# The norms beside a wide attention stage, cut in halves and shared between VectorE, ScalarE and GpSimd

## The chip, the cores and the metric

The kernel runs on one core of one Trainium2 chip. The metric is the device time of one execution in microseconds, the median of several.

## The reference, cut to what matters

The program is a stack of four layers, each an attention and a feed-forward part, over 4 batches of 1024 tokens with 128 channels. The change lies in the last attention (16 heads of 64 channels, "wide") and in what runs beside it:

```
x  = layernorm(x + moe_out(x))          # end of layer 2: inner norm with g2, be2, then + x and a norm
# layer 3 attention
Q, K, V = x @ Wq.T + bq, x @ Wk.T + bk, x @ Wv.T + bv      # 16 heads of 64
w  = softmax(Q K^T * SCALE * adaptive_scale)
y  = x + (w V) @ Wo.T + bo
y  = (y - mean(y)) / sqrt(var(y) + eps) * gamma + beta
x  = layernorm(x + y)
# layer 3 feed-forward: gates by 25 bisection steps over 8 expert logits, then 8 experts
```

So every batch passes two norms before wide attention (inner with g2 and be2, outer after the sum with x) and two after it (inner with gamma and beta, outer after the sum with x).

## The kernel before, in words

`wide_attention` (L3997) treats 32 units, one for each batch and pair of heads; unit u is batch u // 8, pair u % 8. A unit is eight key tiles (kb 0 to 7). All engines walk one list of steps, `plan`, and each executes those that concern it, in the list's order. For each tile and each half of the queries TensorE multiplies scores (L4210 adds the negative maximum, L4213 keys by queries), ScalarE takes the exponential (L4348) into one of six buffers, TensorE weighs the values with it (L4227), and VectorE and GpSimd add up the exponentials of one half each (both L4144). Beside that TensorE computes bf16 scores of the next unit (L3915), of which VectorE takes maxima (`max`, L3946), 16 a unit: three in tiles 0 and 2, two in the others, none in tile 7. In tile 7 the maxima are joined (L3954), transposed by TensorE (L3922), split in a high and a low part (L3959, L3961) and sent by SyncE as a row (`send`). Score, maximum and several other steps share three pairs of PSUM banks in turn, so TensorE waits until the step three places earlier has been read. The next unit but one is projected in tile 6 (q: L3980 on ScalarE, then a cast L3929 on VectorE) and tile 7 (k; v: L3936 on VectorE). Tile 1 holds the sums, tile 3 a reciprocal (L4284), tile 5 the divide (L4279) of the unit before.

GpSimd's add of a tile is placed beside the next tile's first maximum (`add_beside`), since VectorE's maximum reads PSUM.

Three kinds of side work are put into that list:

- `later`: when a batch is finished, its output projection (`rows`, two steps of 32 products each, L249; L256 and L259 on VectorE), its own norms (`stats_1`, `root_1`, `scale_1` in two halves, `affine` three times, `stats_2`, `root_2`, `scale_2` in halves), the turns (four transposes L225, a copy L230), and for batch 0 the routing. One step is taken from it in tiles 0, 2, 4, 6 and 7.
- `rest`: the norms of the layer before for batches 1 to 3 (`Tail.steps`) and, for batches 2 and 3, the gathering of the experts' rows (GpSimd's indirect DMAs, L3285) and their combination (L3298). One step in tiles 2, 4 and 6.
- `work`: the 215 small gate instructions of batch 0, two in each tile once the routing has run (L3750 to L3811).

A norm is eight `bn_stats` and eight `bn_aggr` (`stats_on_dve`, L147, instructions L152 and L155), a reciprocal root by three Newton steps, eleven small instructions (`root_on_dve`, L189), and eight `tensor_scalar` of 128x128 (`scale_on_dve`, L207, instruction L211), all on VectorE. Between the two norms of a batch come three 128x1024 instructions, times gamma, plus beta, plus x: L4307, L4311, L4315 for wide attention's own, L3339, L3342, L3345 for the layer before. Where the steps stand is set by hand:

```
            plan += gate_work(IN_TILE)
            ...
            else:
                plan += next_later()
            if kb in (2, 4, 6) and rest:
                plan.append(rest.pop(0))
```

## Time and profile before

| | us |
|---|---|
| median of 3 runs | 5788.23 (5783.87 to 5794.31) |
| profiled execution | 5795.58, its span 5793.8 |
| TensorE busy | 5261.2, 91% of the span |
| VectorE busy | 4089.6, 71% |
| ScalarE busy | 2696.3, 47% |
| GpSimd busy | 1227.6, 21% |
| granted TensorE clock, mean | 0.946 |
| wide stage, first to last exponential | 3666 to 5239 |

Busy time counts what an engine executes; waits, semaphores and DMA issues are not in it. The shares are means over stages that have different limits, so they say little of the wide stage. In the trace, a row of the timeline gives start and length in us, the engine (DVE is VectorE, ACT ScalarE, POOL GpSimd, PE TensorE), the line, and in brackets how long the engine sat idle before and what released it.

### The profile page before, as it was taken

How to read it: one execution, taken by the hardware profiler on the slowest of the kernel's cores; microseconds unless marked ns; L12 is line 12 of the kernel's file. 1: busy time of each engine (PE TensorE's matmuls, PEld its weight loads, DVE VectorE, ACT ScalarE, POOL GpSimd, SP SyncE). 2: the span in 40 equal slices, each digit the busy share in tenths (PEclk: the TensorE clock that was granted, in tenths of full speed). 3: DMA queues.
4: the chain of work that ended last, by engine and by line, in shares of the span. 5: the costliest groups of instructions: out<-in, count | busy, mean ns of one | idle time of the engine just before them, and what ended most of it. 6: DMA issues, size and time to landing. Idle time of an engine off the chain costs nothing. (4 is left out here: it accounts for less than half of the span.)

```text
span 5793.8 us, 86268 instructions
## 1 busy us (share of the span) xinstructions
PE 5261.2 (91%) x31277; PEld 2629.9 (45%) x31277; DVE 4089.6 (71%) x7068; ACT 2696.3 (47%) x4526; POOL 1227.6 (21%) x859
## 2 busy tenths in 40 slices
PE   6999998787999999989999978899898899997999
PEld 2333333344567777772222248333333333334676
DVE  7888886774677777768898944677787877763412
ACT  4656665221233333337776756444344344442333
POOL 0110100220112322321102203244343233331000
PEclk7999998787989999999999999999999999998999
DMA  4211110002111111112111122000000000001000
GB/s 88 46 31 30 31 30 11 0 0 61 36 33 23 37 23 30 25 23 38 31 31 34 39 60 78 26 16 16 12 19 9 12 12 12 12 12 37 5 4 8
DMA packets 148359, 156.96 MB, mean 27 GB/s; under 512 B 48980, under 2 KB 95108, under 8 KB 147508
## 3 DMA queue, kind: packets, MB, share of 16 engines
q1 hardware_dynamic: 143336, 142.37, 11.3%
q0 software_dynamic: 4096, 8.40, 0.5%
q8 instruction: 250, 4.10, 0.3%
q14 instruction: 173, 1.42, 0.1%
q10 hardware_dynamic: 504, 0.69, 0.1%
HBM read 118.20 MB, written 37.40 MB: 27 GB/s over the span
## 5 line engine op out<-in xcount | busy, mean ns | idle before, releaser
L3946 DVE TENSOR_REDUCE wide_max_parts<-wide_p 128x2 f32<-128x1024 f32 x496 | 592.9, 1218 | 127.9 <-PE wide_p L3915 117.8
L759 ACT ACTIVATE attn_w<-l_p 128x512 f32<-128x512 f32 x1024 | 549.3, 596 | 276.0 <-DVE l_p L1203 152.0
L2518 PE MATMUL caus_p<-caus_x_one,big 128*128 128x129 f32 x4608 | 642.7, 287 | 0.0
L610 DVE TENSOR_REDUCE l_max_parts<-l_p 128x2 f32<-128x1024 f32 x512 | 602.1, 1219 | 46.8 <-PE l_p L586 42.4
L2602 ACT ACTIVATE big<-caus_p 128x512 f32<-128x512 f32 (+3 forms) x768 | 345.9, 489 | 576.7 <-PE caus_p L2504 418.5
L610 DVE TENSOR_REDUCE rot_max_parts<-rot_p 128x2 f32<-128x1024 f32 x488 | 574.1, 1219 | 51.1 <-PE rot_p L586 48.6
L2518 PEld LDWEIGHTS caus_p<-caus_x_one,big 128*128 128x128 f32 x4608 | 592.8, 199 | 35.7 <-issue 2.6
L4213 PE MATMUL wide_p<-arena 64*128 64x512 f32 x2048 | 538.0, 604 | 0.0
L4348 ACT ACTIVATE attn_w<-wide_p 128x1024 f32<-128x1024 f32 x342 | 350.4, 1024 | 390.6 <-PE wide_p L4213 387.1
L4144 POOL TENSOR_TENSOR big<-big,attn_w 128x1024 f32<-128x1024 f32 x128 | 333.5, 2606 | 454.5 <-PE wide_p L3915 442.2
L610 DVE TENSOR_REDUCE caus_max_parts<-caus_p 128x2 f32<-128x1024 f32 (+2 forms) x360 | 340.5, 956 | 24.2 <-PE caus_p L586 15.9
L739 PE MATMUL l_p<-l_q_stack,l_k_stack 98*128 98x512 bf16 x1024 | 336.6, 387 | 13.4 <-ACT attn_w L759 9.6
L4227 PE MATMUL wide_p<-attn_w,arena 128*64 128x512 f32 x1368 | 333.8, 609 | 0.0
L2636 POOL TENSOR_TENSOR attn_w<-attn_w,caus_part 128x256 f32<-128x256 f32 x256 | 186.3, 728 | 685.5 <-DVE caus_part L2578 685.5
L759 ACT ACTIVATE attn_w<-rot_p 128x512 f32<-128x512 f32 x512 | 275.9, 595 | 110.3 <-PE rot_p L739 110.1
L739 PE MATMUL rot_p<-arena 98*128 98x512 bf16 x1024 | 316.1, 389 | 8.1 <-DVE rot_max_lo L638 1.9
L759 ACT ACTIVATE big<-rot_p 128x512 f32<-128x512 f32 x512 | 274.5, 599 | 77.9 <-PE rot_p L739 75.7
L3244 ACT ACTIVATE arena<-moe_experts,moe_b 128x512 f32<-128x512 f32 x256 | 175.3, 687 | 271.3 <-PE moe_experts L3232 271.2
L769 PE MATMUL l_p<-attn_w,l_v_one 128*32 128x512 f32 x2048 | 277.4, 614 | 0.0
L3265 DVE SCALAR_TENSOR_TENSOR x_mid<-moe_experts,last_gates,x_mid 128x128 f32<-128x128 f32 x256 | 72.1, 344 | 279.5 <-PE moe_experts L3254 279.5
L4348 ACT ACTIVATE wide_exps<-wide_p 128x1024 f32<-128x1024 f32 x170 | 174.2, 1024 | 190.9 <-PE wide_p L4213 188.1
L4210 PE MATMUL wide_p<-wide_max_rows,wide_ones_bf 64*128 64x512 bf16 x1024 | 201.6, 390 | 57.0 <-DVE wide_max_parts L3946 50.2
(625 smaller groups left out, 8957.4 us busy)
## 6 DMA issues: line engine op xcount, KB each, us to landing
arena<-q_parts SPq DMA_DIRECT2D x576, 32.0 KB
arena<-k_parts SPq DMA_DIRECT2D x576, 32.0 KB
arena<-inverse_rows SPq DMA_DIRECT2D x64, 256.0 KB
l_q_stack<-q_parts SPq DMA_DIRECT2D x279, 32.0 KB
l_k_stack<-k_parts SPq DMA_DIRECT2D x279, 32.0 KB
q_parts<-arena SPq DMA_DIRECT2D x8, 768.0 KB, 3.6
k_parts<-arena SPq DMA_DIRECT2D x8, 768.0 KB, 3.6
attn_w<-moe_in SPq DMA_DIRECT2D x19, 256.0 KB
```

What stands on the lines that cost most here:

```text
L610: self.nc.vector.tensor_reduce(self.max_parts[:, 2 * p:2 * p + 2, n, half], pair[:, :, 0:self.width(n, half)], AX.X, ALU.max).then_inc(*se ...
L739: mm = nc.tensor.matmul(bank, heads.k_stack[i][0:STACK, j, kb * P:(kb + 1) * P], heads.q_stack[i][0:STACK, j, half * BANK:(half + 1) * BAN ...
L759: self.nc.scalar.activation(self.exps[t % len(self.exps)], bank, ACT.Exp).then_inc(*self.exped.up())
L769: mm = self.nc.tensor.matmul(self.out[self.W * j:self.W * (j + 1), :], self.v_one[u % 2][:, kb, j, :], self.exps[(t + j) % len(self.exps)] ...
L2518: mm = nc.tensor.matmul(outs[o % 2][:, nq % 2 * (C + 1):(nq % 2 + 1) * (C + 1)], exps[h % 2][:, kb, nq * P:(nq + 1) * P], x_one[b % 2][:, ...
L2602: nc.scalar.activation(exps[h % 2][:, kb, lo:BANK], bank[:, lo:BANK], ACT.Exp).then_inc(*exped.up())
L3946: self.nc.vector.tensor_reduce(self.max_parts[:, :, n, h], side, AX.X, ALU.max).then_inc(*self.maxed.up())
L4144: calls.tensor_tensor(to, first, exps[t % E_BUFS], ALU.add).then_inc(*summed[h].up())
L4210: nc.tensor.matmul(side[:, a, :], heads.ones_bf[own[a], :], max_rows[u % 2][own[a], cols], start=True, stop=False)
L4213: mm = nc.tensor.matmul(side[:, a, :], k[u % SLOTS][own[a], kb * P:(kb + 1) * P], q[u % SLOTS][own[a], cols], start=False, stop=True)
L4227: mm = nc.tensor.matmul(out[own[a], h, :], v_tok[u % SLOTS][:, kb, own[a]], exps[t % E_BUFS][:, a, :], start=kb == 0, stop=kb == NT - 1)
L4348: nc.scalar.activation(exps[t % E_BUFS], side, ACT.Exp).then_inc(*exped.up())
```

## The change

All of it is in the wide stage. Batch 3's own norms at the end of the stage are left as they were.

1. `stats_on_dve` can do half of a norm's eight tiles. A list `steps` marks each half as heavy; heavy steps are taken only at two places of a unit: in tile 6 ahead of `project_q`, and in tile 7 between `project_k` and `project_v`.
2. The root stays on VectorE, with one instruction more, which makes `shift` = -mean * rstd. It is taken in tile 0.
3. The scaling goes to ScalarE: `activation(Identity, bias=shift, scale=rstd)`, four 128x128 tiles in tile 2 and four in tile 3.
4. Times gamma, plus beta, plus x go to GpSimd, in tiles 4 and 5 and in tile 0 of the next unit.
5. A norm or a pair of combinations so takes one unit and the next one's first tiles; `rest` is now a list of jobs, in which a batch's own norms stand behind more urgent ones (a job is one batch's; light steps are taken in tiles 0 to 5).
6. The routing of batch 0 moves from unit 11 to unit 14, the gates run beside units 14 to 29, two in each of tiles 0 to 6 and none in tile 7. Gathers stand in tiles 0 and 1, combinations in tiles 6 and 7. `rows` stands in tiles 6 and 7 as before.

```diff
-    def stats_on_dve(self, v, c, src):
+    def stats_on_dve(self, v, c, src, part=None):
         nc = self.nc
-        if c:
+        tiles = range(NT) if part is None else range(part * NT // 2, (part + 1) * NT // 2)
+        if c and part != 1:
             v.wait_ge(*self.out_done.at(NT * c))
-        for i in range(NT):
+        for i in tiles:
...
+class LateNorms:
...
+    def steps(self, b):
+        out = []
+        for second in range(2):
+            out += [(True, ("n_stats", self.tag, b, second, part)) for part in range(2)]
+            out += [(False, ("n_root", self.tag, b, second)), (False, None)]
+            out += [(False, ("n_scale", self.tag, b, second, part)) for part in range(2)]
+            if second == 0:
+                out += [(False, ("n_affine", self.tag, b, i)) for i in range(3)]
+        return out + [(False, ("n_turn", self.tag, c)) for c in range(HALF * b, HALF * (b + 1))]
...
+    def stats_on_dve(self, v, b, second, part, ready):
+        if part == 0:
+            v.wait_ge(*(self.affine.at(3 * b + 3) if second else ready))
+        self.norm.stats_on_dve(v, 2 * b + second, self.x_of(b) if second else self.x1(b), part)
+
+    def root_on_dve(self, v, b, second):
+        norm, c = self.norm, 2 * b + second
+        norm.root_on_dve(v, c)
+        v.wait_ge(*norm.rooted.at(norm.PER_ROOT * (c + 1)))
+        self.nc.vector.scalar_tensor_tensor(self.shift[:, :], norm.mv[:, :, 0], -1.0, norm.rstd[:, :], ALU.mult,
+                                            ALU.mult).then_inc(*self.shifted.up())
+
+    def scale_on_act(self, a, b, second, part):
+        rows = self.x_of(b) if second else self.x1(b)
+        if part == 0:
+            a.wait_ge(*self.shifted.at(2 * (b - self.first) + second + 1))
+        for i in range(part * NT // 2, (part + 1) * NT // 2):
+            self.nc.scalar.activation(rows[:, i, :], rows[:, i, :], ACT.Identity, bias=self.shift[:, i:i + 1],
+                                      scale=self.norm.rstd[:, i:i + 1]).then_inc(*self.norm.out_done.up())
+
+    def affine_on_pool(self, pool, b, i):
...
+        if i == 0:
+            pool.wait_ge(*self.norm.out(2 * b))
+        else:
+            pool.wait_ge(*self.affine.at(3 * b + i))
...
+        self.nc.gpsimd.tensor_tensor(out, one, other, op).then_inc(*self.affine.up())
...
+    def next_step(heavy):
+        while rest and not rest[0]:
+            rest.pop(0)
+        if not rest or rest[0][0][0] != heavy:
+            return []
+        step = rest[0].pop(0)[1]
...
+            if kb == NT - 1:
+                more = u + 2 < len(units)
+                plan += [("project_k", u + 2)] * more + next_step(True) + [("project_v", u + 2)] * more
...
+                if kb == NT - 2:
+                    plan += next_step(True) + [("project_q", u + 2)] * (u + 2 < len(units))
...
-            plan += gate_work(IN_TILE)
+            if kb < NT - 1:
+                plan += gate_work(IN_TILE)
+            if kb < NT - 2:
+                plan += next_step(False)
...
-            else:
-                plan += next_later()
-            if kb in (2, 4, 6) and rest:
-                plan.append(rest.pop(0))
+            if kb >= NT - 2 and ends:
+                plan.append(ends.pop(0))
```

VectorE from the end of one unit into the next, where the first norm of batch 2 of the layer before begins. Before, in units 7 and 8 (L3954 joins the maxima, L3936 writes the values, L3946 are maxima, L4144 adds):

```order
L3929 CAST wide_q_bf<-arena 128x1024
L152 BN_STATS tail_stats<-x_mid 128x6 x8
L155 BN_AGGR tail_mv<-tail_stats 128x2 x8
L3954 TENSOR_REDUCE wide_neg_max<-wide_max_parts 128x16
L3959 CAST wide_max_hi<-wide_p 16x128
L3961 TENSOR_TENSOR wide_max_lo<-wide_p,wide_max_hi 16x128
L3936 TENSOR_TENSOR arena<-wide_p,wide_bv 128x1024
L4144 TENSOR_TENSOR big<-big,attn_w 128x1024
L3946 TENSOR_REDUCE wide_max_parts<-wide_p 128x2 x5
```

With the change, in units 6 and 7 (lines of the changed file: L3991 is the cast, L4016 the join, L3998 the values, L4008 the maxima, L194 the root's first instruction):

```order
L153 BN_STATS tail_stats<-x_mid 128x6 x4
L156 BN_AGGR tail_mv<-tail_stats 128x2 x4
L3991 CAST wide_q_bf<-arena 128x1024
L4016 TENSOR_REDUCE wide_neg_max<-wide_max_parts 128x16
L4021 CAST wide_max_hi<-wide_p 16x128
L4023 TENSOR_TENSOR wide_max_lo<-wide_p,wide_max_hi 16x128
L153 BN_STATS tail_stats<-x_mid 128x6 x4
L156 BN_AGGR tail_mv<-tail_stats 128x2 x4
L3998 TENSOR_TENSOR arena<-wide_p,wide_bv 128x1024
L4216 TENSOR_TENSOR big<-big,attn_w 128x1024
L4008 TENSOR_REDUCE wide_max_parts<-wide_p 128x2 x3
L194 TENSOR_SCALAR tail_std<-tail_mv 128x8
```

The statistics moved from behind the cast, ahead of the join, to ahead of the cast and behind the split; the root follows tile 0's three maxima, where before it stood behind the maxima and the add of tile 2 of unit 8.

GpSimd in units 7 and 8, in which before there are only its adds (L4144) at this place. With the change (L4216 are the adds, L3412 gamma, beta and the sum):

```order
L4216 TENSOR_TENSOR big<-big,attn_w 128x1024
L4216 TENSOR_TENSOR big<-big,wide_exps 128x1024
L3412 TENSOR_TENSOR x_mid<-x_mid,tail_g 128x1024
L4216 TENSOR_TENSOR big<-big,attn_w 128x1024
L3412 TENSOR_TENSOR x_mid<-x_mid,tail_be 128x1024
L4216 TENSOR_TENSOR big<-big,attn_w 128x1024
L4216 TENSOR_TENSOR big<-big,wide_exps 128x1024
L4216 TENSOR_TENSOR big<-big,attn_w 128x1024
L3412 TENSOR_TENSOR x_tok<-x_tok,x_mid 128x1024
```

Three instructions of VectorE now stand between GpSimd's adds, the first two each behind the add of a tile in the middle of the unit.

## Rows read from the trace of the kernel before

Unit u's first tile is counted from its first exponential.

**Rows 1.** Stretches: length, each engine's busy time (instructions), PEclk, DMA share, GB/s.

```profile
3705.99:5070.74 1364.75, 1262.81 (x6524) 492.44 (x6524) 1057.24 (x1481) 581.82 (x579) 525.07 (x221) 0.97 0.05 13
3847.91:4025.74 177.83, 174.21 (x900) 63.61 (x899) 134.69 (x138) 85.20 (x85) 88.89 (x42) 1.00 0.07 18
4741.07:4784.91 43.84, 43.55 (x225) 15.90 (x225) 33.78 (x47) 21.30 (x22) 17.84 (x7) 1.00 0.05 13
4910.14:4939.05 28.91, 28.91 (x199) 20.82 (x197) 11.02 (x18) 7.42 (x7) 6.04 (x3) 1.00 0.01 2
5070.74:5158.03 87.29, 87.20 (x451) 31.93 (x450) 63.49 (x60) 42.60 (x42) 34.96 (x14) 1.00 0.05 13
```

**Rows 2.** Who TensorE waited for in units 1 to 27: us, times, longest.

```profile
PE wide_p L4210 <- DVE wide_max_parts L3946: 48.3, 21, 4.4
PE wide_p L3922 <- DVE wide_neg_max L3954: 32.1, 23, 3.4
```

**Rows 3.** VectorE, unit 28 and into 29: start, us, instruction [idle time before, releaser].

```profile
5100.35 1.22 DVE L4144 TENSOR_TENSOR big<-big,attn_w 128x1024 f32<-128x1024 f32 x1
...
5106.05 1.22 DVE L4279 TENSOR_TENSOR arena<-arena 128x1024 f32<-128x1024 f32 x1
5107.19 2.38 DVE L3946 TENSOR_REDUCE wide_max_parts<-wide_p 128x2 f32<-128x1024 f32 x2
...
5113.36 0.69 DVE L3929 CAST wide_q_bf<-arena 128x1024 bf16<-128x1024 f32 x1 [2.66 <-ACT arena L3980]
...
5118.19 1.23 DVE L3936 TENSOR_TENSOR arena<-wide_p,wide_bv 128x1024 f32<-128x1024 f32 x1 [3.00 <-PE wide_p L3901]
...
5126.44 1.23 DVE L3946 TENSOR_REDUCE wide_max_parts<-wide_p 128x2 f32<-128x1024 f32 x1 [1.32 <-PE wide_p L3915]
```

**Rows 4.** GpSimd in the same unit, in order of time.

```profile
5097.95 2.36 POOL L4144 TENSOR_TENSOR big<-big,wide_exps 128x1024 f32<-128x1024 f32 x1 [2.21 <-PE wide_p L3915]
...
5109.63 3.28 POOL L4144 TENSOR_TENSOR big<-big,wide_exps 128x1024 f32<-128x1024 f32 x1
```

**Rows 5.** VectorE in units 7 and 8: a statistics step and a root.

```profile
4025.32 1.64 DVE L152 BATCH_NORM_STATS2 tail_stats<-x_mid 128x6 f32<-128x128 f32 x8
4026.87 0.62 DVE L155 BATCH_NORM_AGGREGATE tail_mv<-tail_stats 128x2 f32<-128x6 f32 x8
...
4051.73 0.17 DVE L193 TENSOR_SCALAR tail_std<-tail_mv 128x8 f32<-128x8 f32 x1
...
4052.14 2.30 DVE L199 TENSOR_TENSOR tail_square<-tail_rstd 128x8 f32<-128x8 f32 x1
...
4055.97 2.35 DVE L3946 TENSOR_REDUCE wide_max_parts<-wide_p 128x2 f32<-128x1024 f32 x2
```

**Rows 6.** ScalarE between the exponentials of tiles 3 and 4, unit 28.

```profile
5097.70 1.02 ACT L4348 ACTIVATE attn_w<-wide_p 128x1024 f32<-128x1024 f32 x1 [2.25 <-PE wide_p L4213]
```

**Rows 7.** Stretches: tile 4 of unit 8; tiles 1 to 3 of units 9 and 28.

```profile
4053.08:4059.83 6.75, 4.64 (x26) 1.55 (x24) 6.48 (x13) 2.05 (x3) 2.37 (x2) 1.00 0.00 0
4102.65:4118.17 15.52, 15.48 (x86) 5.00 (x84) 13.88 (x29) 7.74 (x8) 4.71 (x3) 1.00 0.01 3
5078.90:5094.42 15.52, 15.47 (x86) 5.01 (x84) 11.88 (x11) 7.74 (x8) 4.71 (x3) 1.00 0.01 2
```

**Rows 8.** Groups of instructions, xcount | busy us, mean ns | idle before (whole span; PE units 1 to 27).

```profile
L3155 POOL TENSOR_TENSOR x_mid<-x_mid,rot_g 128x1024 f32<-128x1024 f32 x4 | 9.4, 2348 | 296.9 <-DVE x_mid L211 296.9
...
L1856 ACT ACTIVATE lin_o_scale<-lin_o_scale,lin_eps 128x128 f32<-128x128 f32 x4 | 1.6, 402 | 10.0 <-DVE lin_o_scale L1718 10.0
...
L225 PE MATMUL wide_p<-ident,x_tok 128*128 128x128 f32 x48 | 7.5, 283 | 0.3 <-DVE wide_max_parts L3946 0.3
L1988 PE MATMUL wide_p<-wide_w_router,x_chn 128*128 128x8 f32 x16 | 1.8, 251 | 0.0
```

**Rows 9.** GpSimd and VectorE side by side in unit 11, in order of time.

```profile
4239.51 2.74 POOL L4144 TENSOR_TENSOR big<-big,wide_exps 128x1024 f32<-128x1024 f32 x1
...
4239.95 3.38 DVE L4279 TENSOR_TENSOR arena<-arena 128x1024 f32<-128x1024 f32 x1
```

More of the change, by code:

```diff
@@ L4037, in wide_attention, with gathered @@
     IN_TILE = 2
-    work, later, rest = [], [], tail.steps(1)
-    for b in range(2, nb):
-        chunks = [c for c, (route, at) in enumerate(back.chunks) if (route.first_tile + at) // NT == b]
-        rest += [("gather", chunks[0])]
-        for c in chunks:
-            rest += [("gather", c + 1)] if c < chunks[-1] else []
-            rest += [("none",), ("combine", c)]
-        rest += tail.steps(b)
+    mine = LateNorms(st, "own", norm, turn, gamma[:, :], beta[:, :], affine, lambda b: mid, 0)
+    moe = LateNorms(st, "moe", tail.norm, tail.turn, tail.g2[:, :], tail.be2[:, :], tail.affine,
+                    lambda b: core.x_mid[:, b * NT:(b + 1) * NT, :], 1)
+    norms = {"own": mine, "moe": moe}
+    def gathered(b):
+        first = [c for c, (route, at) in enumerate(back.chunks) if (route.first_tile + at) // NT == b][0]
+        return [(heavy, (kind, first + c)) for heavy, kind, c in (
+            (False, "gather", 0), (False, "gather", 1), (True, "combine", 0), (True, "combine", 1),
+            (False, "gather", 2), (False, "gather", 3), (True, "combine", 2), (True, "combine", 3))]
+    work, ends, later = [], [], []
+    rest = [moe.steps(1)] + [gathered(b) + moe.steps(b) for b in range(2, nb)]
     def gate_work(n):
@@ L4103, in wide_attention @@
                     finish(units[u - 1][0])
-            else:
-                plan += next_later()
-            if kb in (2, 4, 6) and rest:
-                plan.append(rest.pop(0))
-    while work or later:
-        plan += gate_work(1) + next_later()
+            if kb >= NT - 2 and ends:
+                plan.append(ends.pop(0))
+    assert not work and not any(rest) and not ends
     last = len(units) - 1
@@ L4113, in wide_attention @@
     finish(nb - 1)
-    while later:
-        plan += next_later()
+    plan += ends + later
     plan = with_banks(plan, 3, {
@@ L4120, in wide_attention @@
         "turn": lambda c: (turn.kept, c + 1),
-        "tail_turn": lambda c: (tail.turn.kept, c + 1),
+        "n_turn": lambda tag, c: (norms[tag].turn.kept, c + 1),
         "route": lambda: (entmax.router.done, 1), **heads.released()})
@@ L4325, in _ @@
                     back.on_dve(v, *args)
-                elif kind == "tail":
-                    b = args[1]
-                    tail.on_dve(v, *args, back.combined.at(NT * (b - 1)))
+                elif kind == "n_stats":
+                    tag, b, *part = args
+                    norms[tag].stats_on_dve(v, b, *part, rows.out(2 * b + 1) if tag == "own" else
+                                            back.combined.at(NT * (b - 1)))
+                elif kind == "n_root":
+                    norms[args[0]].root_on_dve(v, *args[1:])
                 elif kind == "route":
```

55 lines of the change are left out of this document (34 added, 21 removed).

## Prediction

> **What bounds the kernel now.** I read the trace by stretches of the wide stage first. One attention unit (one batch, one pair of heads) is eight key tiles, and the stage is 32 units. Units 28 and 29, beside which no norm, gate or gather runs, take 87.29 us with TensorE busy for 87.20 of it, so the floor is 43.65 us a unit and TensorE sets it [rows 1]. Units 1 to 27, beside which all the side work lies, take 1364.75 us, where 27 x 43.65 = 1178.6 would do: **186.2 us** over the floor. What ends TensorE's waits there is VectorE: 48.3 us for the maxima that free a score bank and 32.1 for the joined maximum of the next unit [rows 2]. TensorE's busy time is also above its floor, 1262.8 against 27 x 43.6 = 1177.2, partly extra matmuls, partly the granted clock: 0.97 over these units, 1.00 in the clean ones [rows 1]. So VectorE's queue, not its 77% of busy time, is what to look at.
>
> The clean unit tells where VectorE has room [rows 3]. It has none between the divide and the maxima of tile 6 (5107.19, with no idle time before them), but before the cast of q in tile 6 it sits idle for 2.66 us, before the values of tile 7 for 3.00, and before the first maximum of tile 1 for 1.32. Before the change the norm steps lie in tiles 2, 4 and 6, or behind the cast: in unit 7 the statistics (1.64 and 0.62) stand between the cast and the join [rows 5], so TensorE's transpose of the join comes as much later.
>
> **What can't go.** The projections of one batch (the rows step) take 28.91 us where the two tiles that hold them take 6.26 + 8.16 = 14.42 in a clean unit (tiles 7 and 0: of 43.65, tiles 1 to 3 take 15.52 [rows 7] and tiles 4 to 6 three times 4.57, which is how far the adds at 5100.35 and 5104.92 stand apart, the second being 1.13 ahead of the divide [rows 3]): 14.5 us of TensorE's own, three times, 43.5 [rows 1]. Twelve turns are 48 transposes of together 7.5 us, of which I count 7.0, and the router's matmuls are 1.8 [rows 8]. That is 52.3. **186.2 - 52.3 = 133.9 us** is what side work costs the stage now, and the most that the change can bring.
>
> **The change, part by part.**
> - *Statistics in halves*, in 12 units, before the cast in tile 6 and before the values in tile 7. Half of 1.64 + 0.62 is 1.13 us [rows 5], under 2.66 and 3.00 [rows 3]. They read one SBUF tensor, and their 8 instructions took 1.64 whoever else ran. Cost 0; without that cover it would be 24 x 1.13.
> - *Root* in tile 0, 12 times: eleven small instructions of 0.17 and one more for the shift, at a pitch of 0.20, 2.4 us. The idle time behind is 1.32, so tile 1's maxima come 1.1 us late (1.5 where two gate steps stand ahead). TensorE bears that: the root of unit 8 held VectorE from 4051.73 to 4055.97, 4.2 us, and the tile that followed took 6.75 in place of 4.57 [rows 5, 7], so about 2.0 us of lateness are free. And statistics of 2.3 us at just this place in unit 9 cost nothing, its tiles 1 to 3 taking 15.52 as in unit 28 [rows 7]. Cost 0, bound 12 x 0.4.
> - *The root's neighbours.* In unit 8 one instruction of the root took 2.30 us and not 0.17, because a GpSimd add ran beside it [rows 5]. In tile 0 GpSimd's add ends before the third maximum does. No such wait.
> - *Scaling on ScalarE*, four instructions in tile 2 and four in tile 3. The nearest row (128x128, SBUF to SBUF) has 0.40 each, 1.6 in all [rows 8]; between two tiles' exponentials ScalarE idles 2.25 us [rows 6]. Cost 0. VectorE loses 96 such instructions.
> - *Gamma, beta and sum on GpSimd*, in 6 units: two in tiles 4 and 5, one in the next unit's tile 0. The same instructions ran there in an earlier stage at 2.35 us [rows 8]. Here is the price. GpSimd's add of tile 4 ends at 5100.31, and behind it the new instruction starts 0.14 later; VectorE's add begins at 5100.35 and so is first [rows 3, 4]. Where both want the second SBUF input, one stands still: GpSimd's add of 5109.63 took 3.28, that is 2.2 after VectorE's ended [rows 4], and a divide that began beside GpSimd took 3.38, until 1.1 after it [rows 9]. With these two: gamma ends 5103.8; GpSimd's add 3.9 to 6.3; VectorE's add, due at 5104.92, ends 7.4; beta, waiting since 6.4, goes ahead of the divide and ends 9.6; the divide ends 10.7; tile 6's maxima start 3.4 us late. Less the 2.0 that are free, **1.4 us** in each of units 1, 7 and 11. In units 17, 21 and 26 two gate steps stand behind each add, and one of them waits out one more instruction, 2.3 to 2.6: 6.0 late, 4.0 lost, and some at a lower clock, 5. Together 3 x 1.4 + 3 x 5 = **19 us**. Bounds: nothing below (gathers that put GpSimd as far behind in units 4 to 7 cost 3.2 us in 177.83, so near 0 is possible), and above 12 instructions that each hold VectorE twice for 2.3, less 6 x 2: 43. I take the worked value, since its two durations are rows of exactly this meeting. The third, in tile 0, starts behind GpSimd's add when VectorE is on maxima, which read PSUM: 0.
> - *Combines* in tiles 6 and 7, eight in pairs. Units 4 to 7 now lose 177.83 - 174.6 = 3.2 us to three of them [rows 1]. The four in tile 7 lie in the 3.00; the four in tile 6 stand before the cast but behind GpSimd's long add: 0.8 each, **3 us** (0 to 4.3).
> - *Gates*: none in tile 7, same number. Unit 21 has two in each tile and takes 43.84, so 0.19 over 15.5 units, **3 us** (0 to 6).
> - *Gathers* in tiles 0 and 1, where GpSimd idles; in unit 14 one slips to tile 2: **2 us** (0 to 4).
>
> - *The new waits.* ScalarE's first scaling waits for the root's shift; behind it stand the exponentials, and for them TensorE. The shift is made two tiles earlier (tile 0 against 2), so it would have to be over 5 us late to be felt. GpSimd's gamma waits for the last scaling, one tile before; behind it stand GpSimd's own adds, and an exponential waits for those only six buffers, three tiles, on. TensorE's turn waits for the scaling of the tile before, due some 4 us ahead. Cost 0 each, as long as the roots stay in tile 0; SyncE's queue is not touched.
>
> Sum: 133.9 - 19 - 3 - 3 - 2 = 107 us less. The profiled execution took 5795.6, so 5688.6; it stands 7.4 above the median of the three runs, so against that median I forecast **5681 us**.
>
> The Trainium skill (GPSIMD Engine Reference, its summary of when to use which engine) says that two-input elementwise work belongs on VectorE, GpSimd being about twice as slow. The trace agrees on the ratio, 2.35 against 1.22 [rows 3, 8]. By that rule the move of 18 instructions would be a loss of 18 x 1.13 = 20 us and not a gain; an estimate, and one that holds only where GpSimd is waited for, which here it is only through the shared input.
>
> **The rivals.**
> - *GpSimd is never in the way* (13%). If the new instruction always loses the race and VectorE's next add comes after it, the price of 19 falls to about 0: 5788.2 - 133.9 + 8 = 5662. For it: VectorE starts 0.1 us earlier in the row. Against: in rows 9 the instruction that had waited went first. The Trainium skill (SBUF — State Buffer, "Who interferes with whom") has whoever issues first hold the shared pair for its whole instruction; that would give VectorE the first add and GpSimd the turn after it, which is the forecast's chain.
> - *The blocking spreads* (17%). Both bounds are reached, 43 + 4 + 6 + 4 and 5 for the roots: 62, so 5788.2 - 72 = 5716. For it: in the gated units two more steps stand behind each add, and VectorE once late stays beside GpSimd. Against: units 4 to 7.
> - *The excess was not the norms'* (4%). Gates and combines alone, in units 12 to 14, would be what is slow; then half stays: 5788.2 - 67 = 5721.
> - *Slower* (4%). Each of the 18 GpSimd instructions holds two adds in turn, and the add held on GpSimd's side makes the next tile's late too, three tiles on: if that costs 9 us per instruction, 162, then 5788.2 - 134 + 8 + 162 = 5824. It decides from 7 us per instruction on ((134 - 8) / 18). Against: a single wait is 2.3 us, and there is 2.66 + 3.00 of idle time twice a unit to recover in.
>
> **How the numbers follow.** Forecast 62%, the others 13, 17, 4 and 4. The range takes in the first two rivals and nearly the third: 5655 to 5722. A measurement of this kernel can tell 0.2%, 11.6 us, from no change. Faster by more than that: 0.93; within: 0.03; slower: 0.04.
>
> **What would show it.** Right: units with only statistics, roots and scaling near 43.7 to 44; TensorE's wait for the join and for maxima below 25 us together, and the granted clock near 1.00 in the stage; VectorE's divide stretched to 3 us in units 1, 7, 11, 17, 21 and 26 and nowhere else; four activations of 0.4 us or less between exponentials. Wrong: stretched adds in units without gamma and beta; an exponential that waits for GpSimd; statistics in tile 6 that delay the cast; tile 1 longer than 4.98 us behind a root.

## The result, and the profile after the change

The changed kernel takes **5696.59 us** (median of 4 runs, 5692.06 to 5699.48), the kernel before on the same chip 5791.27 (4 runs, 5783.87 to 5795.12): ratio 0.984, 95% interval 0.9827 to 0.9853, or 94.7 us less. The profiled execution took 5694.58, its span 5692.8. The forecast was 5681.

Runs of this kernel also differ ahead of the wide stage: its first exponential came between 3648.4 and 3678.8 us in the profiled executions of this study, with the same instructions ahead of it. So beside the times I compare the **stage** alone: from the first exponential of its first tile to the first exponential of its last. It took 1568.43 us before and takes 1475.27 now, 93.2 less. That is nearly all of the 94.7.

Units are cut at the first exponential of their first tile from here on. Those of [rows 1] were cut one exponential earlier, at the last of the unit before, because the load of the activation table had been counted as the first. For sums over units that matters little: before, units 1 to 27 are 184.2 us over the floor of 43.65 a unit by the right cut, where the prediction had 186.2.

Stretches of the changed kernel: units 1 to 27; unit 2; units 14 and 15; unit 17; units 28 and 29 (length, busy time of each engine and instructions, granted clock, DMA share, GB/s).

```profile
3704.09:4975.19 1271.10, 1237.43 (x6517) 482.32 (x6515) 1001.73 (x1357) 614.71 (x665) 565.26 (x239) 0.99 0.05 14
3750.16:3793.81 43.65, 43.61 (x228) 15.96 (x225) 33.87 (x46) 21.30 (x22) 19.79 (x8) 1.00 0.04 13
4297.80:4399.72 101.92, 92.70 (x469) 34.50 (x467) 85.09 (x103) 42.61 (x43) 55.03 (x30) 0.97 0.09 22
4457.85:4508.13 50.28, 45.37 (x228) 16.36 (x225) 43.76 (x57) 24.36 (x30) 22.37 (x9) 0.97 0.04 11
4975.19:5063.85 88.66, 88.33 (x460) 32.71 (x458) 68.11 (x93) 46.84 (x53) 34.93 (x14) 1.00 0.05 13
```

Units 1 to 27 take 1271.10 where [rows 1] had 1364.75: 92.6 over the floor. The granted clock rose from 0.97 to 0.99. Unit 2, which has the sum of a norm in its tile 0 and the statistics of the next in tiles 6 and 7, stands exactly on the floor. Apart from what can't go, what is left sits in few places: unit 17 is 6.6 over the floor, units 14 and 15 together 14.6 (1.9 of that is the router).

Who TensorE waited for in units 1 to 27 (us in total, times, longest).

```profile
PE wide_p L4282 <- DVE wide_max_parts L4008: 17.0, 7, 3.8
PE wide_p L3984 <- DVE wide_neg_max L4016: 8.1, 17, 1.0
PE wide_p L3968 <- DVE wide_max_parts L4008: 7.3, 5, 2.4
```

The first two answer to [rows 2]: the wait for maxima fell from 48.3 to 17.0, that for the join from 32.1 to 8.1 and from 3.4 to 1.0 at the longest. The third, a wait of the projections, was 17.0 before.

VectorE from unit 0 into unit 1: a whole norm's statistics in two halves, then the root.

```profile
3693.85 0.47 DVE L153 BATCH_NORM_STATS2 tail_stats<-x_mid 128x6 f32<-128x128 f32 x2
...
3696.19 0.69 DVE L3991 CAST wide_q_bf<-arena 128x1024 bf16<-128x1024 f32 x1 [1.60 <-ACT arena L4042]
...
3697.95 0.85 DVE L153 BATCH_NORM_STATS2 tail_stats<-x_mid 128x6 f32<-128x128 f32 x4
...
3701.03 1.23 DVE L3998 TENSOR_TENSOR arena<-wide_p,wide_bv 128x1024 f32<-128x1024 f32 x1 [1.94 <-PE wide_p L3963]
...
3704.30 3.66 DVE L4008 TENSOR_REDUCE wide_max_parts<-wide_p 128x2 f32<-128x1024 f32 x3 [0.91 <-PE wide_p L3977]
3707.87 0.16 DVE L194 TENSOR_SCALAR tail_std<-tail_mv 128x8 f32<-128x8 f32 x1
...
3710.08 0.17 DVE L3393 SCALAR_TENSOR_TENSOR wide_shift_moe<-tail_mv,tail_rstd 128x8 f32<-128x8 f32 x1
3710.16 2.35 DVE L4008 TENSOR_REDUCE wide_max_parts<-wide_p 128x2 f32<-128x1024 f32 x2
```

The halves lie in idle time: of 2.66 us before the cast 1.60 is left, of 3.00 before the values 1.94 [rows 3]. The root runs from 3707.87 to 3710.16 without a stretched step (in [rows 5] one took 2.30), and the next exponentials stand 4.98 and 5.56 us apart (3709.07, 3714.63) as in a clean unit. On ScalarE the scaling takes 1.64 for four:

```profile
3715.92 1.02 ACT L4423 ACTIVATE attn_w<-wide_p 128x1024 f32<-128x1024 f32 x1 [0.27 <-PE wide_p L4285]
3716.84 1.64 ACT L3401 ACTIVATE x_mid<-x_mid,wide_shift_moe,tail_rstd 128x128 f32<-128x128 f32 x4
3719.61 1.02 ACT L4423 ACTIVATE wide_exps<-wide_p 128x1024 f32<-128x1024 f32 x1 [1.13 <-PE wide_p L4285]
```

The exponential behind it still waits 1.13 for TensorE, so the scaling costs nothing.

**Where it does cost.** GpSimd in unit 1, tiles 3 to 6, with gamma at 3726.75 and beta at 3732.36 (L3412):

```profile
3724.43 2.36 POOL L4216 TENSOR_TENSOR big<-big,wide_exps 128x1024 f32<-128x1024 f32 x1 [2.21 <-PE wide_p L3977]
3726.75 2.35 POOL L3412 TENSOR_TENSOR x_mid<-x_mid,tail_g 128x1024 f32<-128x1024 f32 x1
3729.06 3.35 POOL L4216 TENSOR_TENSOR big<-big,attn_w 128x1024 f32<-128x1024 f32 x1
3732.36 3.44 POOL L3412 TENSOR_TENSOR x_mid<-x_mid,tail_be 128x1024 f32<-128x1024 f32 x1
3735.76 3.33 POOL L4216 TENSOR_TENSOR big<-big,attn_w 128x1024 f32<-128x1024 f32 x1
3739.23 3.27 POOL L4216 TENSOR_TENSOR big<-big,wide_exps 128x1024 f32<-128x1024 f32 x1
```

VectorE beside it:

```profile
3726.83 3.35 DVE L4216 TENSOR_TENSOR big<-big,attn_w 128x1024 f32<-128x1024 f32 x1
...
3732.37 1.21 DVE L4216 TENSOR_TENSOR big<-big,attn_w 128x1024 f32<-128x1024 f32 x1
3733.50 3.38 DVE L4351 TENSOR_TENSOR arena<-arena 128x1024 f32<-128x1024 f32 x1
3736.81 2.34 DVE L4008 TENSOR_REDUCE wide_max_parts<-wide_p 128x2 f32<-128x1024 f32 x2
...
3741.34 1.72 DVE L3991 CAST wide_q_bf<-arena 128x1024 bf16<-128x1024 f32 x1 [1.05 <-ACT arena L4042]
```

Gamma starts 0.04 us before the end that its predecessor shows, and 0.08 ahead of VectorE's add at 3726.83. That add then takes 3.35 in place of 1.22, until 1.1 after gamma's end. VectorE's next add begins 0.01 behind beta, and this time it is beta that stands still (3.44 in place of 2.35); but the divide behind that add begins while beta still runs, and takes 3.38, until 1.1 after beta's end. So tile 6's maxima start at 3736.81, 3.1 us late by the distances of [rows 3], and tile 6 is 1.5 us longer.

The unit is 2.4 over the floor, though. The other 0.9 is in tile 7 and comes through something that the prediction did not have: GpSimd's add of tile 6, at 3739.23, now lies beside VectorE's cast of q, which takes 1.72 in place of 0.69, and the join stands behind the cast. The cast is held in units 1, 7 and 11 and in no other unit; in the kernels below in which it takes 0.69 there, tile 7 is on the floor.

In a gated unit (17) two gate steps of 0.2 us stand behind the late add, and each is held as well. At 1.22 and 0.2 each the three would be over some 1.6 us after 4480.58, near 4482.2; the maxima start at 4488.39, 6.2 late, and tile 5 is 4.5 us longer. The divide is held behind that (3.37), and tile 6 is another 1.9 longer.

```profile
4480.58 3.35 DVE L4216 TENSOR_TENSOR big<-big,wide_exps 128x1024 f32<-128x1024 f32 x1
4483.85 2.32 DVE L3863 COPY_PREDICATED wide_ent_low<-wide_ent_keep,wide_ent_mid 128x8 f32<-128x8 uint32 x1
4486.21 2.26 DVE L3849 TENSOR_SCALAR wide_ent_width<-wide_ent_width 128x8 f32<-128x8 f32 x1
4488.39 2.34 DVE L4008 TENSOR_REDUCE wide_max_parts<-wide_p 128x2 f32<-128x1024 f32 x2
```

TensorE stands still behind them, and its next matmuls of scores take 1.61 for four. In unit 2, where the granted clock is 1.00, they take 1.02 (at 3750.38); over unit 17 it is 0.97.

```profile
4489.66 0.39 PE L4282 MATMUL wide_p<-wide_max_rows,wide_ones_bf 64*128 64x512 bf16 x2 [3.83 <-DVE wide_max_parts L4008]
4489.89 1.61 PE L4285 MATMUL wide_p<-arena 64*128 64x512 f32 x4
```

The second dear place is unit 14, where four gathers stand ahead of GpSimd's adds and the first gates stand in VectorE's queue. GpSimd, then VectorE:

```profile
4317.60 0.94 POOL L3286 DMA_INDIRECT x_mid<-moe_out,sort_index  x1 [0.30 <-issue]
4318.56 2.71 POOL L4216 TENSOR_TENSOR big<-big,attn_w 128x1024 f32<-128x1024 f32 x1
```

```profile
4318.99 2.31 DVE L3841 TENSOR_TENSOR wide_ent_width<-wide_ent_high,wide_ent_low 128x8 f32<-128x8 f32 x1
...
4325.67 2.38 DVE L3816 SCALAR_TENSOR_TENSOR wide_ent_power<-wide_ent_diff 128x64 f32<-128x64 f32 x1
...
4331.62 2.33 DVE L3845 TENSOR_SCALAR wide_ent_f_low<-wide_ent_f_low 128x8 f32<-128x8 f32 x1
```

The gathers push GpSimd's add from beside a maximum (which reads PSUM) to beside a gate step (which reads SBUF); 0.2 us of work becomes 2.3, VectorE is late by then, and the pair meets again in each of the next tiles. The first meeting costs TensorE nothing; then tiles 4, 5 and 6 are 0.5, 1.4 and 4.1 us longer.

### The profile page after: what moved, and what is told of

Same layout as the page of the kernel before. It is cut to its first block and busy times, and to the rows that moved or that the text cites. A ratio compares the mean times of both kernels' runs of the same rounds, so it can differ in the third digit from the quotient of the medians.

```text
span 5692.8 us, 86280 instructions
## 1 busy us (share of the span) xinstructions
PE 5238.4 (92%) x31277; PEld 2622.7 (46%) x31277; DVE 4035.5 (71%) x6966; ACT 2733.3 (48%) x4622; POOL 1266.8 (22%) x877
## 5 line engine op out<-in xcount | busy, mean ns | idle before, releaser
L4008 DVE TENSOR_REDUCE wide_max_parts<-wide_p 128x2 f32<-128x1024 f32 x496 | 595.4, 1220 | 129.5 <-PE wide_p L3977 117.4
L4216 POOL TENSOR_TENSOR big<-big,attn_w 128x1024 f32<-128x1024 f32 x128 | 331.8, 2592 | 391.9 <-PE wide_p L3977 379.4
L611 DVE TENSOR_REDUCE caus_max_parts<-caus_p 128x2 f32<-128x1024 f32 (+2 forms) x360 | 340.6, 956 | 24.2 <-PE caus_p L587 15.9
L740 PE MATMUL l_p<-l_q_stack,l_k_stack 98*128 98x512 bf16 x1024 | 336.9, 388 | 12.8 <-ACT attn_w L760 9.0
L2637 POOL TENSOR_TENSOR attn_w<-attn_w,caus_part 128x256 f32<-128x256 f32 x256 | 186.2, 727 | 681.9 <-DVE caus_part L2579 681.9
L3233 PE MATMUL moe_experts<-x_chn,big 128*128 128x512 f32 x512 | 237.1, 606 | 14.0 <-ACT arena L3245 8.8
```

The costliest lines, as they stand in the source:

```text
L611: self.nc.vector.tensor_reduce(self.max_parts[:, 2 * p:2 * p + 2, n, half], pair[:, :, 0:self.width(n, half)], AX.X, ALU.max).then_inc(*se ...
L740: mm = nc.tensor.matmul(bank, heads.k_stack[i][0:STACK, j, kb * P:(kb + 1) * P], heads.q_stack[i][0:STACK, j, half * BANK:(half + 1) * BAN ...
L3233: self.nc.tensor.matmul(self.up_banks[o % 3], self.w1[:, e, c * P:(c + 1) * P], cols, start=True, stop=True).then_inc(*self.up_mm.up())
L4008: self.nc.vector.tensor_reduce(self.max_parts[:, :, n, h], side, AX.X, ALU.max).then_inc(*self.maxed.up())
L4216: calls.tensor_tensor(to, first, exps[t % E_BUFS], ALU.add).then_inc(*summed[h].up())
```

## The experiments

Ten kernels, each the changed kernel with one edit (or, the best one, three). All in one table; the stage and the excess over the floor in units 1 to 27 are of the profiled execution, the ratio is to the kernel before on the same chip, with its 95% interval.

The kernels did not all run on one chip (the kernel before had medians of 5788.76, 5788.93 and 5791.64 beside the later ones), and most of the intervals overlap. So I compare these kernels with each other by the stage, unit by unit. That is one profiled execution of each, but units that an edit does not touch agree to 0.05 us in nearly all cases. The exceptions are unit 5 (up to 0.2), units 14 and 15, which together lie between 14.3 and 15.9 over the floor in kernels that are edited elsewhere, and the last two units. Differences between stages of up to 1.5 us therefore mean nothing.

| kernel | median us | ratio | stage us | units 1 to 27 |
|---|---|---|---|---|
| before | 5791.27 | | 1568.43 | 184.2 |
| changed | 5696.59 | 0.984 (0.9827 to 0.9853) | 1475.27 | 92.6 |
| gamma, beta, sum on VectorE | 5685.21 | 0.9828 (0.9797 to 0.9859) | 1465.23 | 82.5 |
| all three in tile 0 of the next unit | 5680.52 | 0.9821 (0.979 to 0.9852) | 1462.95 | 80.5 |
| gates from unit 16 on | 5687.63 | 0.9828 (0.9796 to 0.986) | 1463.05 | 80.4 |
| clearings in place of gamma and beta | 5670.57 | 0.9802 (0.9761 to 0.9843) | 1451.45 | 68.7 |
| scaling on VectorE | 5753.63 | 0.9945 (0.9923 to 0.9966) | 1534.03 | 144.4 |
| tile 6's half behind the cast | 5704.0 | 0.9859 (0.9827 to 0.9892) | 1489.54 | 105.8 |
| statistics whole, ahead of the cast | 5703.17 | 0.9858 (0.9825 to 0.9891) | 1475.09 | 92.4 |
| spare tensor_scalar on VectorE | 5773.39 | 0.9972 (0.9956 to 0.9987) | 1547.64 | 158.8 |
| spare bn_stats on VectorE | 5708.9 | 0.9874 (0.9811 to 0.9938) | 1486.43 | 101.3 |
| best | 5654.79 | 0.9775 (0.9754 to 0.9797) | 1437.98 | 55.3 |

### What do gamma, beta and the sum cost, and through what?

**Back on VectorE**, in the same tiles.

```diff
-        self.nc.gpsimd.tensor_tensor(out, one, other, op).then_inc(*self.affine.up())
+        self.nc.vector.tensor_tensor(out, one, other, op).then_inc(*self.affine.up())
```

> The change with one part undone: gamma, beta and the sum run on VectorE again, at the same places of the list (tiles 4 and 5, tile 0 of the next unit); halves of statistics and ScalarE's scaling stay. In the changed kernel the six units with these steps and the tile behind them take 25 us over the floor of 43.65 a unit. Theory A (VectorE waits for GpSimd at the shared second SBUF input): each instruction costs VectorE 1.13 us of its own, 2.3 in tiles 4 and 5 together, little more than the 2.0 us of lateness that TensorE bears; so 0 to 1 us in units 1, 7 and 11 and 1 to 3 in units 17, 21 and 26, about 8 in all, and the kernel 17 us faster than the changed one, ratio 0.981 to before. Theory B (VectorE is full in these tiles, whoever holds it up): 1.13 us more work costs as much as a wait; no faster than the changed kernel, ratio 0.984.

Measured: 1.7 us each in units 1, 7 and 11, and 4.0, 3.9 and 3.7 in the gated units 17, 21 and 26 (16.5 in all) where the GpSimd version has 26.1. Twice what I expected, yet 10 less than on GpSimd. In unit 17 of this kernel neither add is held; only the divide, at 4478.37, meets GpSimd's add and takes 3.39. The meeting happens once and not twice, and no gate step stands in it. The same one is left in the other five units (in unit 1 the divide, at 3726.80, takes 3.38).

**All three in tile 0 of the next unit**, still on GpSimd, back to back behind its add.

```diff
-                out += [(False, ("n_affine", self.tag, b, i)) for i in range(3)]
+                out += [(False, None)] * 2 + [(False, ("n_affine", self.tag, b))]
...
-                    norms[args[0]].affine_on_pool(pool, *args[1:])
+                    for i in range(3):
+                        norms[args[0]].affine_on_pool(pool, args[1], i)
```

> All three of gamma, beta and the sum stay on GpSimd but stand together in tile 0 of the next unit, where GpSimd idles about 8 us behind its add and VectorE mostly reads PSUM; tiles 4 and 5 hold none. Theory A: three instructions are 7.2 us and end before tile 2; VectorE's only two-input work there is the add of tile 1 and, in units 18, 22 and 27, gate steps. Cost 0 in units 2, 8 and 12, up to 1 us in the gated ones; 25 us of excess shrink to under 4, the kernel about 21 us faster than the changed one (5696.6), ratio 0.980. Theory B: the same amount of work on GpSimd costs the same wherever it stands, 25 us, ratio 0.984.

Measured: 0 in the ungated units (1, 2, 7, 8, 11 and 12 stand on the floor), but 4.2 to 4.4 in each of the units 18, 22 and 27, where gates run. The stage lost 12.3 us, not the 21 expected. In unit 18 VectorE reads:

```profile
4501.44 3.28 DVE L4216 TENSOR_TENSOR big<-attn_w 128x1024 f32<-128x1024 f32 x1
4504.64 2.34 DVE L3863 COPY_PREDICATED wide_ent_low<-wide_ent_keep,wide_ent_mid 128x8 f32<-128x8 uint32 x1
4507.01 0.17 DVE L3849 TENSOR_SCALAR wide_ent_width<-wide_ent_width 128x8 f32<-128x8 f32 x1
```

and GpSimd beside it:

```profile
4501.27 2.36 POOL L3412 TENSOR_TENSOR x_tok<-x_tok,x_mid 128x1024 f32<-128x1024 f32 x1
4504.60 2.35 POOL L4216 TENSOR_TENSOR big<-attn_w 128x1024 f32<-128x1024 f32 x1 [0.97 <-PE wide_p L3977]
```

In a gated unit the add of tile 1 begins 0.17 after the sum and is held until 1.1 after it; then a gate step, begun 0.04 after GpSimd's add, is held for the whole of that. The add is held as long in the ungated units 2, 8 and 12 (3.24 us each), which stand on the floor, and in units 18, 22 and 27 of the best version below (3.2 to 3.3), which has no gates at that place and loses 0.2 to 0.3 there. What costs 4 us is the gate step held behind it.

**Clearings in place of gamma and beta.** GpSimd writes zeros over the rows for about as long (1.96 and 0.52 us) and reads nothing; the inner norm's result is zero in this kernel, and the sum stays.

```diff
+        if i < 2:
+            for rows in (x1, x1):
+                self.nc.gpsimd.memset(rows, 0.0).then_inc(*self.cleared.up())
+                pool.wait_ge(*self.cleared.now())
+            self.nc.gpsimd.memset(x1[:, 0:NT // 2, :], 0.0).then_inc(*self.affine.up())
+            return
```

> A measurement, with part of the computation changed: times gamma and plus beta (tiles 4 and 5) are replaced by two and a half clearings of the same 128x1024 rows on GpSimd, so that the inner norm's output is zero. GpSimd is busy about as long (2 x 0.95 + 0.5 us, plus two waits on itself, some 2.6 in place of 2.35), but reads no SBUF. The sum in tile 0 is left. Theory A (shared read): VectorE's add in tile 4 takes 1.22 and not 3.35, the divide 1.22 and not 3.38; what is left is GpSimd's own adds, 0.3 to 0.6 us late. Excess of the six places 25 us to under 6. Theory B (GpSimd's queue is late): GpSimd's adds start as late as in the changed kernel, VectorE waits for them, and the excess stays above 15 us.

Measured: units 1, 7 and 11 on the floor, units 17, 21 and 26 at 0.2 to 0.3, the gates' own price: 25.3 us gone in these six units, 23.8 in the stage. GpSimd in unit 1 is as late as before:

```profile
3728.25 1.96 POOL L3415 MEMSET x_mid<- 128x1024 f32 x2
3730.27 0.52 POOL L3417 MEMSET x_mid<- 128x512 f32 x1
3730.76 2.36 POOL L4223 TENSOR_TENSOR big<-big,attn_w 128x1024 f32<-128x1024 f32 x1
```

and VectorE's adds, one of which lies wholly beside the clearings, are short:

```profile
3728.35 1.22 DVE L4223 TENSOR_TENSOR big<-big,attn_w 128x1024 f32<-128x1024 f32 x1
...
3732.91 1.29 DVE L4223 TENSOR_TENSOR big<-big,attn_w 128x1024 f32<-128x1024 f32 x1
```

So it is reading SBUF that costs; GpSimd's longer queue by itself costs nothing. This is what the Trainium skill (SBUF — State Buffer, "Who interferes with whom") states of a VectorE instruction with two SBUF inputs: it contends with a GpSimd instruction that reads, not with one that only writes.

### Why are units 14 and 15 dear?

The gates begin in unit 16, behind the gathers and combines that stand in units 14 and 15, still two a tile, and end in unit 31.

```diff
-            if kb < NT - 1:
+            if kb < NT - 1 and u >= 16:
                 plan += gate_work(IN_TILE)
```

> The gates of batch 0 begin in unit 16 and not in unit 14, still two a tile, and so run into unit 31; nothing else moves. In the changed kernel units 14 and 15, where gates, gathers and combinations meet, lie 13.6 us over the floor, 1.9 of it the router. If the cost is that meeting (each small gate step waits 2.3 us for a GpSimd that the gathers made late), units 14 and 15 come to 1.9 + 1.0 us, as units 4 to 6 cost 1.0 with gathers and combinations alone, and the kernel is 9 to 10 us faster, ratio 0.982. If the gathers and combinations cost it by themselves, 13.6 stays and the ratio is 0.984. Two gate steps a tile in units 30 and 31 should cost under 1 us.

Measured, units 14 and 15 in one stretch:

```profile
4306.16:4396.23 90.07, 88.99 (x469) 33.67 (x466) 74.21 (x77) 42.57 (x43) 53.25 (x30) 1.00 0.09 25
```

90.07 in place of 101.92, which is 2.8 over the floor: the router's 1.9 and 0.9 for gathers and combines. The clock is 1.00, where it was 0.97. The stage is 12.2 us shorter; the gathers are still there. Gathers and combines without gates cost 0.9 here, gates without them 0.2 in a unit; dear is only both in one unit. (Moving the gathers and leaving the gates was not tried.)

### Do the three parts that cost nothing matter?

**The scaling back on VectorE**, in the same tiles 2 and 3.

```diff
+    def scale_on_vector(self, v, b, second, part):
+        rows = self.x_of(b) if second else self.x1(b)
+        self.norm.scale_on_dve(v, 2 * b + second, rows, rows, part)
```

> The last scaling of each half goes back from ScalarE to VectorE, in tiles 2 and 3; gamma, beta and the sum stay on GpSimd. The stage of the changed kernel lasts 1475.3 us, 92.6 of it above the floor in units 1 to 27. If VectorE's queue is what these tiles have too little of, the 12 norms give back 1.1 us of work in each of two tiles with little idle time, and now and then a wait on GpSimd: 12 to 36 us more, ratio to the kernel before 0.986 to 0.990. The rival, that the place of the scaling never mattered: 0 more, ratio 0.984.

Measured: 58.8 us more, well outside what either theory gave; nearly two thirds of the whole gain is gone. In unit 3 (50.29 us where it was 44.82) VectorE and GpSimd read:

```profile
3805.41 1.21 DVE L4220 TENSOR_TENSOR big<-big,wide_exps 128x1024 f32<-128x1024 f32 x1
3806.55 3.27 DVE L212 TENSOR_SCALAR x_tok<-x_tok,tail_mv,tail_rstd 128x128 f32<-128x128 f32 x4
```

```profile
3806.86 2.36 POOL L4220 TENSOR_TENSOR big<-big,wide_exps 128x1024 f32<-128x1024 f32 x1 [2.63 <-PE wide_p L3981]
```

Four instructions of 0.33 take 3.27, since GpSimd's add begins 0.3 after the first: one of the four waits it out. This is so in 19 of the 24 groups of the stage; in the kernel before, where the groups stood elsewhere, 5 of the same 96 instructions took over 1.3. That left a question: is it this meeting, the 1.1 us of work, or something that hangs on the scaled rows? Two kernels settle it. The scaling stays on ScalarE, and VectorE gets idle instructions at the same 24 places, which no one waits for.

```diff
+    def beside_on_vector(self, v):
+        spare, spared = self.spare
+        for i in range(4):
+            if spared.total > 1:
+                v.wait_ge(*spared.at(spared.total - 1))
+            self.nc.vector.tensor_scalar(spare[:, i % 2, :], self.core.ident[:, :], self.shift[:, 0:1],
+                                         self.shift[:, 1:2], ALU.subtract, ALU.mult).then_inc(*spared.up())
...
+                elif kind == "n_scale":
+                    norms[args[0]].beside_on_vector(v)
```

> The changed kernel, whose scaling stays on ScalarE, with four idle tensor_scalar of 128x128 added on VectorE at each of the 24 places of a half scaling in tiles 2 and 3; they read a constant and write a spare tile, and no one waits for them. The scaling on VectorE cost 58.8 us more than 12 to 36 expected, and 19 of its 24 groups held one instruction of 2.4 us. If the meeting with GpSimd's add is what costs, these four cost the same: 45 to 60 us more in the stage than 1475.3, most groups with one instruction above 2 us, ratio to the kernel before 0.992 to 0.995. If VectorE's lost 1.1 us by itself is what costs, or what hangs on the scaling's result, the stage is longer by 10 to 25 us.

The second has five of these in place of the four:

```diff
+            self.nc.vector.bn_stats(spare[:, i, :6], self.core.ident[:, :]).then_inc(*spared.up())
```

> The same with five bn_stats of 128x128 in place of the four tensor_scalar: about the same time of VectorE (5 x 0.2 us), but one SBUF input and no instruction that has been seen to wait for GpSimd. If the meeting is what costs: 0 to 15 us more than a stage of 1475.3, no stretched instruction in the groups, ratio to the kernel before 0.984 to 0.987. If the lost time is what costs, as much as with the tensor_scalar, whatever that is.

Durations of the spare instructions (ns, least, median, longest), the tensor_scalar beside the norms of the layer before and the own ones:

```profile
L3401 DVE TENSOR_SCALAR wide_spare<-ident,wide_shift_moe x48: 332/335/2504, 3729.8 to 4630.3; 128x128 f32<-128x128 f32 x48
L3401 DVE TENSOR_SCALAR wide_spare<-ident,wide_shift_own x48: 331/336/2511, 4213.1 to 5077.2; 128x128 f32<-128x128 f32 x48
```

and the bn_stats:

```profile
L3401 DVE BATCH_NORM_STATS2 wide_spare<-ident x120: 269/276/290, 3726.4 to 5012.0; 128x6 f32<-128x128 f32 x120
```

The tensor_scalar cost 72.4 us (45 to 60 expected), 23 of the 96 above 2.1 us; about the same amount of VectorE's time in bn_stats costs 11.2, and none of the 120 is stretched. Why the idle tensor_scalar cost 14 us more than the scaling itself is open; four more of them were held.

The 11.2 are not the price of the bn_stats' own time either. In units 1, 3, 7, 9, 11 and 13 they cost nothing. 10.9 us lie in units 17, 21, 26 and 28, where gates run, and there they moved other instructions beside GpSimd's adds: in unit 28 a gate step, at 5016.52, takes 2.28 and the divide, at 5022.80, takes 2.83, where the changed kernel has none held. Work in tiles 2 and 3 is free where it brings no meeting.

A meeting costs more than the 2.1 us that it adds to an instruction. In unit 3 two of them cost 5.5 us with the scaling on VectorE: TensorE stands still 3.7 us longer, and it is busy for 1.8 us longer (46.55 against 44.77) with the granted clock at 0.97 in place of 1.00.

**The place of the statistics**: tile 6's half behind the cast, as before.

```diff
-                    plan += next_step(True) + [("project_q", u + 2)] * (u + 2 < len(units))
+                    plan += [("project_q", u + 2)] * (u + 2 < len(units)) + next_step(True)
```

> Tile 6's half of the statistics is put behind the cast again, as in the kernel before; all else stays as changed. If the place in VectorE's queue is what matters, tile 7 (or 6) is later by about the 1 us that half a norm's statistics take, in each of 12 norms: 12 us more, ratio to the kernel before 0.986. The rival, that halving alone does it: 0 more, ratio 0.984.

Measured: 14.3 us more, but not all of it is the statistics. The edit moves whatever heavy step tile 6 takes, and in units 4, 5, 14 and 15 that is a pair of combines: 3.9 us of the 14.3, 2.5 of them in unit 15. The statistics themselves cost 0.9 to 1.0 in each of ten units, 9.9 in all. In units 8 and 16, beside the rows step, their half stays in tile 6 and costs nothing. The place matters, for both.

**The halves**: both parts in tile 6 ahead of the cast.

```diff
-            out += [(True, ("n_stats", self.tag, b, second, part)) for part in range(2)]
+            out += [(True, ("n_stats", self.tag, b, second))]
```

> The statistics of a norm are taken whole (2.26 us), ahead of the cast in tile 6, where VectorE stands idle 2.66 us in an ungated unit. If only the place counts: 0 more in the ungated units, 0 to 0.5 us in each gated one, 0 to 3 us in all, ratio 0.984. The rival, that the halves are needed: the cast is late by about 1 us in each of 12 norms, 12 us more, ratio 0.986.

Measured: a stage of 1475.09 against 1475.27, no unit different by more than 0.1. The halving brings nothing; the 2.66 us hold the whole. (Its median is above the changed kernel's, but its profiled run already began the stage 18 us later, where no instruction differs: the times alone would not have told these two kernels apart.)

### A better version

```diff
-            if kb < NT - 1:
-                plan += gate_work(IN_TILE)
+            alone = kb < 2 and rest and rest[0] and rest[0][0][1] and rest[0][0][1][0] == "n_affine" or busy == u
+            if kb == 0:
+                busy = u if alone else -1
+            if kb < NT - 1 and u >= 16 and not (busy == u and kb < 2):
+                plan += gate_work(2 * IN_TILE if u == len(units) - 1 else IN_TILE)
```

and gamma, beta and the sum in tile 0, as above.

> A version meant to be better: gamma, beta and the sum of a norm stand together on GpSimd in tile 0 of the next unit, the gates, gathers and combines begin in unit 16 instead of unit 14, and the three gated units into which such a sum falls have no gates in their tiles 0 and 1, and unit 31 has four a tile. If the three costs are separate, the first saves 12.3 us and the second 12.2, as each did alone, and the third the 4.2 to 4.4 us in each of three units: 37 us less than the changed kernel, a stage of about 1438 us, time about 5660 us, ratio to the kernel before 0.9775. The rival, that the gated units lose the same wherever the sum stands: 24 to 25 us less, ratio 0.980.

Measured: a stage of 1437.98 us (1438 expected), 5654.79 in the median (5 runs, 5648.58 to 5663.28), 2.25% under the kernel before; the stage is 37.3 us shorter than that of the changed kernel. Units 1 to 27, and who TensorE waited for in them, the only one left:

```profile
3708.01:4941.85 1233.84, 1227.73 (x6517) 479.88 (x6515) 959.58 (x1319) 614.27 (x665) 553.16 (x239) 1.00 0.06 15
```

```profile
PE wide_p L3984 <- DVE wide_neg_max L4016: 4.7, 14, 0.5
```

55.3 over the floor and 1.4 in unit 28, of which 52.3 can't go: side work costs the stage 4.4 us now, where it cost some 132 before.

## Why the prediction was right, and where it was not

- **The floor and what can't go**: right. The rows step costs 14.5 us in each of units 8, 16 and 24; the turns 1.2 in each of six units (the last is unit 28), 7.0; the router 1.9.
- **Statistics, root, scaling at 0**: right, and for the reasons given. The last two experiments show the cost of the other places: 9.9 for half of ten norms' statistics behind the cast, 58.8 for the scaling on VectorE. The latter I had not priced; I wrote only that VectorE loses 96 instructions. Halving, part of the change's idea, brought nothing.
- **Gamma, beta and sum, 19 us**: measured 26.1, less the gates' 0.2 in three units 25.4 (2.4 each in units 1, 7 and 11, forecast 1.4; 6.4, 6.5 and 5.3 in units 17, 21 and 26, forecast 5). Clearing in their place gave back 23.8. The mechanism was the shared input, as put. The step that failed is "behind it the new instruction starts 0.14 later; VectorE's add begins at 5100.35 and so is first". The 0.14 of [rows 4] is there because GpSimd's add of one tile waits for its own add of the tile before; gamma waits for nothing that is late, starts as its predecessor ends, and is first by 0.08. The chain that followed (who is held, in what order) was therefore another one, with a similar lateness by luck: tile 6's maxima were 3.1 late (3.4 forecast) and cost 1.5 (1.4 forecast). What makes 2.4 of it is a term that the sum did not have, the cast of q held by GpSimd's add, 0.9 us in tile 7. In unit 17 the 6.0 of lateness were 6.2, and the held divide behind them came on top.
- **The two rivals beside it.** "GpSimd is never in the way" fell. "The blocking spreads" put these instructions at 43 and did not come either: 25.4 lies nearer to 19.
- **Gathers, 2 us (0 to 4), and gates**: the largest miss. Units 14 and 15 cost 14.6, 12.8 without the router, where gathers and the gates and combines of these two units had some 4. I had looked at gathers and gates apart, and unit 21, from which I took the gates' price, has no gathers. Apart they are cheap: gates from unit 16 on cost about 0.2 a unit (2.2 in all), and with no gates beside them gathers and combines cost 0.4 in each of units 14 and 15. Together they meet as gamma does with gates, and the experiment without gates there gave back 12.2.
- **Combines, 3 us**: about 1.0 (0.4 and 0.6 in units 4 and 5, 0 in 6).
- **Sum**: 27 us of new costs forecast, 41.4 found by these items (25.4, 12.8, 1.0, 2.2); a gain of 107 forecast for the stage, 93.2 measured. The median missed by 15.6: 13.8 from the stage, the rest is how the runs before it scatter.
- **The signs I named**: the granted clock 0.99 (near 1.00 said); the waits of [rows 2] 25.1 together (below 25 said), with 7.3 more on a line of their kind; the tiles at the root 4.98 and 5.56 us, as in a clean unit; no exponential waited for GpSimd. The divide is stretched in units 1, 7, 11 and 17 as said (and in unit 31, as before the change), but not in 21 and 26, where adds and gate steps are. One of the signs against me did appear, stretched adds of VectorE in units without gamma and beta: 2.57 in units 4 and 5 and 2.56 in unit 15, behind the gathers, with a combine of 2.44 in each. In units 4 and 5 they cost next to nothing. In unit 14 it was gate steps that were held.
- The Trainium skill's advice (GPSIMD Engine Reference, "Engine selection": two-input elementwise work to VectorE), which I had weighed as a loss of 20 us by engine speed, does not decide here: on VectorE these instructions cost 10 us less, in another place on GpSimd 12.3 less, and clear of the gates there nothing.

## What to carry to other kernels

Before moving work to GpSimd, or leaving it on VectorE, write down which VectorE instructions beside it read SBUF in a form that was seen held (adds, products, tensor_scalar, casts, predicated copies), and put GpSimd's reading beside VectorE's PSUM reads or its statistics; the place was worth more than the engine, and tiny instructions are the worst neighbours, since each can cost a whole GpSimd instruction. Price two kinds of side work together in each unit where both run, not each from a unit that has only one. And measure a stage from its own first to last instruction when runs scatter upstream of it.

## What the runs showed of the hardware that I had not expected

- Of two waiting instructions back to back on GpSimd the second starts with the end of the first (3726.75 after 3724.43 + 2.36) and keeps the shared input from a VectorE add that begins 0.08 later. When it depends on its predecessor it starts later: by 0.14 for the adds of [rows 4], by 0.08 for the sum behind beta in tile 0 (4501.27 after 4498.81 + 2.38).
- Hundredths decide. In the wide stages of the twelve profiles an add or divide of VectorE began between 0.5 us ahead of a 128x1024 instruction of GpSimd and 0.01 behind it 379 times: each time GpSimd's took 3.0 us or more and VectorE's at most 1.23. It began 0.02 to 0.5 behind 73 times, and 67 times it was VectorE's that was held. The Trainium skill's rule on the shared pair (same page and section as above: whoever issues first has it for its whole instruction), which the page words for VectorE's two-port modes, holds for these as well; it is in who is first that I erred.
- Even instructions on 128x8 elements, 0.17 us by themselves, stand for 2.26 to 2.34 us beside a GpSimd instruction, a TENSOR_SCALAR and a COPY_PREDICATED among them, while 120 bn_stats at such places never took more than 0.29.
- 1.1 us of tensor_scalar placed 24 times cost 58.8 and 72.4 us of the stage, the same time in bn_stats 11.2, nearly all of it where gates run.
